# Two layers of attention and mixture on one core: the stage borders opened, and the closing norm moved into the attention's last stretch

## What is computed

```python
x = L0_attn_x                                    # [4, 1024, 256]
x = x + attn0(layernorm(x))                      # 16 heads, window of 64 keys, softmax, W_out
x = x + ffn0(layernorm(x))                       # softmax gate + bias over 8 experts, top 2, SwiGLU; 2 shared experts
x = x + attn1(layernorm(x))
x = x + ffn1(layernorm(x))                       # gate logits, 8 Sinkhorn rounds, each expert takes its top tokens

def attn1(x, ...):                               # here x is the normalised input
    Q, K, V = x @ wq + bq, x @ wk + bk, x @ wv + bv
    attn = softmax(Q @ K.T / 4)                  # heads by a reshape of [4*16, 1024, 16], all keys
    out = ctx @ wo + bo + x
    mu, var = mean(out), var(out)
    return (out - mu) * rsqrt(var + 1e-5) * gamma + beta
```

## Time and profile before

| what | us |
|---|---|
| median of 3 runs (lowest, highest) | 2432.5 (2428.86, 2436.8) |
| the profiled execution | 2439.18 |
| its span, first to last instruction | 2437.2 |
| TensorE busy | 2024.1 (83%) |
| VectorE busy | 1630.2 (67%) |
| ScalarE busy | 1116.2 (46%) |
| GpSimd busy | 452.3 (19%) |

### The profile page before, as it was taken

The page is one execution under the profiler, slowest core; times in us unless marked ns, Lnnn a source line. Parts: engine busy times, 40 slices in busy tenths (PEclk is TensorE's granted clock), DMA queues, the critical chain, the costliest instruction groups (busy, mean ns, idle before and its releaser), DMA issues. The chain is left out here.

```text
span 2437.2 us, 51300 instructions
## 1 busy us (share of the span) xinstructions
PE 2024.1 (83%) x18407; PEld 1393.6 (57%) x18408; DVE 1630.2 (67%) x2834; ACT 1116.2 (46%) x2169; POOL 452.3 (19%) x608
## 2 busy tenths in 40 slices
PE   2888888669979999989968899999999999835052
PEld 2766766448879999988857533434334343324042
DVE  3666666556735555546644579999999999386953
ACT  1555545333223333332223158888888888611010
POOL 2101001010011111114434112112221122030036
PEclk9999999889989999999989769999999999955566
DMA  2000000192151111113339777745755900031036
GB/s 87 2 0 0 0 0 0 60 336 80 35 182 47 47 47 47 47 43 106 109 114 271 201 51 72 67 46 52 49 47 47 71 2 2 5 104 35 0 112 200
DMA packets 207045, 172.15 MB, mean 71 GB/s; under 512 B 121740, under 2 KB 184808, under 8 KB 204744
## 3 DMA queue, kind: packets, MB, share of 16 engines
q1 hardware_dynamic: 187448, 131.64, 27.8%
q0 software_dynamic: 17744, 26.26, 4.0%
q10 hardware_dynamic: 1728, 12.58, 1.4%
HBM read 106.30 MB, written 63.84 MB: 70 GB/s over the span
## 5 line engine op out<-in xcount | busy, mean ns | idle before, releaser
L1811 DVE TENSOR_REDUCE ga_nmax<-banks 128x1 fp32r<-128x1024 f32 x512 | 615.5, 1219 | 39.8 <-PE banks L1890 38.4
L1845 ACT ACTIVATE ga_probT<-banks 128x512 f32<-128x512 f32 x1024 | 556.7, 597 | 157.6 <-PE banks L1903 105.9
L1890 PE MATMUL banks<-a_ks,a_qs 48*128 48x512 f32 x1024 | 392.3, 466 | 9.3 <-PEq L77 5.3
L1903 PE MATMUL banks<-a_qs,a_ks 49*128 49x512 f32 x1024 | 381.8, 453 | 0.0
L1920 PE MATMUL banks<-ga_probT,a_v 128*32 128x256 f32 x4096 | 332.9, 398 | 6.4 <-ACT ga_o L1851 6.4
L1890 PEld LDWEIGHTS banks<-a_ks,a_qs 48*128 48x128 f32 x1024 | 159.4, 195 | 225.2 <-DVE ga_nmax L1811 158.3
L1321 PEld LDWEIGHTS banks<-rb_xT,rb_own_w 128*128 128x128 f32 x2272 | 267.1, 193 | 8.3 <-issue 3.7
L1321 PE MATMUL banks<-rb_xT,rb_own_w 128*128 128x128 f32 x2272 | 267.9, 276 | 4.1 <-DMA rb_w<-in_L_ffn_rw_dram 3.5
L1790 POOL DMA_DIRECT2D a_qs<-ga_max_rows x256 | 130.8, 519 | 580.6 <-DVE ga_max_rows L1818 539.4
L1296 ACT ACTIVATE rb_silu<-banks,rb_own_b 128x128 f32<-128x128 f32 x284 | 80.9, 367 | 254.9 <-PE banks L1321 254.9
L1920 PEld LDWEIGHTS banks<-ga_probT,a_v 128*32 128x32 f32 x4096 | 81.6, 108 | 198.3 <-ACT ga_probT L1845 151.2
(11 more groups left out here) (288 smaller groups left out, 3031.7 us busy)
## 6 DMA issues: line engine op xcount, KB each, us to landing
m_xnT<-xnT_parts ACTq DMA_DIRECT2D x12, 1024.0 KB, 4.8
sorted_out<-rb_yb SPq DMA_DIRECT2D x71, 128.0 KB, 1.7
xnT_parts<-np_parts SPq DMA_DIRECT2D x8, 1024.0 KB, 9.2
m_w<-in_L_ffn_rw_dram SPq DMA_DIRECT2D x2, 4096.0 KB, 21.6
values<-pg_v SPq DMA_DIRECT2D x16, 512.0 KB, 3.1
a_v<-values SPq DMA_DIRECT2D x16, 512.0 KB, 9.1
a_qs<-queries_rounded SPq DMA_DIRECT2D x28, 256.0 KB, 8.5
a_ks<-keys_rounded SPq DMA_DIRECT2D x28, 256.0 KB, 9.6
```

The costliest lines, as they stand in the source:

```text
L1811: nc.vector.tensor_reduce(nmax[b % 2][:, at:at + 1], slot[:], axis=AX.X, op=ALU.max, negate=True).then_inc(use_read, 1)
L1845: nc.scalar.activation(probT[k % SETS][2 * h + n][:], b_t[ring_place["weights", w] % RING][:], ACT.Exp, scale=SCALE).then_inc(exp_ready, 1)
L1890: return nc.tensor.matmul(slot[:, HALF * kh:HALF * (kh + 1)], qs[a][rows, n, P * q:P * (q + 1)], ks[a][rows, n, HALF * kh:HALF * (kh + 1)] ...
L1903: nc.tensor.matmul(bank[:], ks[a][rows, 2 * gp + n, P * kt:P * (kt + 1)], qs[a][rows, 2 * gp + n, HALF * hf:HALF * (hf + 1)], start=True, ...
```

## The change

Nothing is computed in another way except the last gate; work and waits are placed elsewhere.

1. `setup` loses its stage: `window_attention` loads x (batch 0, then the qkv weights, then the other batches) and takes statistics of the first 8 tiles before its steps, of the other 24 in places 0 to 5 of step 0, and finishes them at place 6. The wide mask is made for one pair and copied. TensorE waits for the identity first, and for weights and masks where they are used.
2. `finish_stats` is gone. Its operations (`Closing`) stand at the start of `normalised_tiles`, `project_groups` and `gated_tiles`, and inside `group_attention`.
3. `normalised_tiles` writes the first two parts straight into the buffers of the next stage, and no longer waits for its writes; `shared_expert` 0 waits for them where it reuses memory (SP before it loads weights, VectorE before `gated`, ScalarE before `silus`).
4. The weights of `project_groups` are loaded during `shared_expert` 1.
5. In `group_attention` the statistics are taken right after each `project`. From step 512 on VectorE finishes those of 28 tiles, and in eight chosen steps does `new_x` (scale, multiply, add old x) and new statistics by four tiles; GpSimd adds beta. The old x is loaded into a free query buffer in blocks 27 to 31.
6. `gated_tiles` takes the place of `norm_residual`: it does the last four tiles, and then normalise, transposes, gate matmuls with the gate's 8 columns stationary and 512 tokens moving, and transposes of the logits.

```diff
@@ window_attention, SP, VectorE
+            load_x(0)
             sp.dma_start(wqkv[:], ...).then_inc(wqkv_in, 16)
+            for b in range(1, B):
+                load_x(b)
...
+            nc.vector.memset(eps[:], LN_EPS)
+            for t in range(TB):
+                tile_statistics(t)
+            finish(0, 0, TB)
             dve.wait_ge(w_hi, ONE + 1)
...
+                    if c == 0 and place < 6:
+                        for t in range(TB + 4 * place, TB + 4 * place + 4):
+                            tile_statistics(t)
+                    if c == 0 and place == 6:
+                        finish(1, TB, T)
@@ window_attention, ScalarE, TensorE
+                        if c == 0 and place == UP - 1:
+                            root(1, TB, T)
                         weights(r, c, place)
...
-            pe.wait_ge(w_in, ONE + 16 * HU * 2)
-            pe.wait_ge(w_cut, ONE + 1)
-            pe.wait_ge(consts_set, ONE + 1)
+            pe.wait_ge(ident_set, ONE + 1)
@@ normalised_tiles, SP
-                if i == 5:
-                    sp.wait_ge(parts_kept, ONE + 16 * 4)
-                    for s in range(2):
-                        shared.load_chunk(sp, xnT_out, s, s, chunks_in)
...
-            sp.wait_ge(chunks_in, ONE + 16 * 2)
-            sp.wait_ge(parts_kept, ONE + 16 * STEPS)
-            for u in range(2):
-                sp.wait_ge(rows_kept[u], ONE + 16 * (STEPS // 2))
@@ shared_expert, SP
+            if route is not None:
+                sp.wait_ge(shared.parts_kept, 16 * NC)
+                for kept in shared.rows_kept:
+                    sp.wait_ge(kept, 16 * NC // 2)
+            else:
+                sp.wait_ge(w_ready, ONE + 2)
+                project.load(sp, ins, routed_in)
@@ project_groups
-            dve.wait_ge(b_in, ONE + B_IN)
-            dve.wait_ge(v_one, ONE + 2)
+            closing.on_vector(dve)
...
-            act.wait_ge(b_in, ONE + B_IN)
+            closing.on_scalar(act)
...
-            pe.wait_ge(w_in, ONE + W_IN)
@@ group_attention
+        XB_AT, QUARTER = (27, 28, 30, 31), T // 4
+        NEW_AT = [UNITS + k for k in (3, 7, 14, 18, 22, 26, 30, 34)]
...
+            def new_x(i):
+                for t in range(4 * i, 4 * i + 4):
+                    nc.vector.scalar_tensor_tensor(g.x[:, t, :], g.x[:, t, :], g.mean[:, t:t + 1], gamma[:],
+                                                   ALU.subtract, ALU.mult).then_inc(scaled_ready, 1)
+                dve.wait_ge(xb_in[4 * i // QUARTER], ONE + 16)
+                dve.wait_ge(scaled_ready, ONE + 4 * i + 4)
+                for t in range(4 * i, 4 * i + 4):
+                    nc.vector.scalar_tensor_tensor(g.x[:, t, :], g.x[:, t, :], g.rstd[:, t:t + 1], kept_tiles(qs, t, 1)[:, 0],
+                                                   ALU.mult, ALU.add).then_inc(x_ready, 1)
+
+            def new_statistics(i):
+                dve.wait_ge(beta_ready, ONE + i + 1)
+                for t in range(4 * i, 4 * i + 4):
+                    nc.vector.bn_stats(g.stats[:, t, :], g.x[:, t, :])
...
-                        if arg >= LATE:
-                            dve.wait_ge(use_read, ONE + use + 1)
-                            statistics(arg)
-                if UNITS <= s < UNITS + LATE:
...
+                        dve.wait_ge(use_read, ONE + use + 1)
+                        for h in range(2):
+                            nc.vector.bn_stats(g.stats[:, t + 2 * h, :], g.x[:, t + 2 * h, :]).then_inc(stats_ready, 1)
+                if s == UNITS:
+                    dve.wait_ge(stats_ready, ONE + READY)
+                    closing.moments(dve, 0, 0, READY)
+                if s == NEW_AT[0]:
+                    dve.wait_ge(ends_in, ONE + 16 * 3)
+                    closing.inverses(dve, 0, 0, READY)
+                if s in NEW_AT:
+                    i = NEW_AT.index(s)
+                    if i < READY // 4:
+                        new_x(i)
+                    if i:
+                        new_statistics(i - 1)
...
+                if back == UNITS - LAG + 3:
+                    closing.on_scalar(act, 0, 0, READY)
...
+            for i in range(READY // 4):
+                pool.wait_ge(x_ready, ONE + 4 * i + 4)
+                four = g.x[:, 4 * i:4 * i + 4, :]
+                nc.gpsimd.tensor_tensor(four, four, beta[:].unsqueeze(1).broadcast_to([P, 4, D]), ALU.add).then_inc(beta_ready, 1)
@@ gated_tiles in place of norm_residual: VectorE, ScalarE, TensorE
+            closing.moments(dve, 0)
+            closing.inverses(dve, 0)
+            normalise(0)
+            normalise(1)
+            last_tiles()
+            closing.moments(dve, 1, READY)
+            closing.inverses(dve, 1, READY)
+            for i in range(2, STEPS):
+                normalise(i)
...
+                for k in range(KD):
+                    last = nc.tensor.matmul(b_g[i % 2][0:E, :], gw[:, k, :], xnT[i % 2][:, k, :], start=(k == 0), stop=(k == KD - 1))
...
+                for c in range(C):
+                    last = nc.tensor.transpose(b_l[i % 2][:, E * c:E * (c + 1)], lT[i % 2][:, P * c:P * (c + 1)], g.ident[0:E, 0:E])
...
+            for i in range(STEPS + 2):
+                if i < STEPS:
+                    transposes(i)
+                if 1 <= i <= STEPS:
+                    gates(i - 1)
+                if i >= 2:
+                    turned(i - 2)
```

488 lines of the change are left out of this document (258 added, 230 removed).

## The result

The changed kernel took 2353.2 us (median of four runs, 2347.5 to 2367.3) against 2434.7 for the kernel before (2428.9 to 2439.4): a ratio of 0.9681, 95% interval 0.9658 to 0.9704. That is 10 us more than the 81.5 between the medians: it sets the shortest of four runs after against one of the longest before.

The account below looks back on a forecast made before the run. It took TensorE and VectorE as nearly full in the score stage, and the closing norm and gate as a chain of waits. Terms -16 - 12 - 9 + 3 + 13.4 - 46 = -67 gave a median of 2366 us, range 2342 to 2386.

Parts of the forecast that it names:

- Start, -16: Kernel start: first qkv matmul 23 us earlier, 7 us given back in step 0; 16 us saved, between 12 and 20.
- Gate stage, -12: First mixture's gate stage: shared expert's first matmul at 517.5 instead of 529.33; 12 us saved, bounds 8 and 15.
- I take 3 us for the compute: First mixture's gate stage: 3 us saved in compute, part of SP's last issue ending at about 511 instead of 514.6.
- a wait that only moves behind this stage: First mixture's gate stage: SP's queue ends no earlier, ScalarE waits to 525; 8 of 12 us lost, 2374; chance 0.08.
- Projection stage, -9: Projection stage: weights already there, so VectorE's 9.97 us wait shrinks; 9 us saved, bounds 7 and 9.5.
- Score stage, +3: Score stage: added VectorE statistics delay scores by 0.2 us at 14 projections; 3 us lost, bounds 0 and 13.
- the slower rival: Score stage: late maxima keep TensorE's clock low for 160 us or more longer, losing at least 67 us; chance 0.03.
- Stretch without scores, +13.4: Stretch without scores: added new_x and statistics groups of 5.85 us make the last context late; 13.4 us lost, bounds 8 and 20.
- ScalarE's root costs it two table loads and itself, 2 x 1.28 + 0.3 = 2.9: Stretch without scores: the root takes 2.9 us of ScalarE, which sets the pace, putting projection 14 at 2101.3.
- Closing stage, -46: Closing norm and gate: last tiles, then six low-clock steps and a tail, ending at 2193; 46 us saved.
- I take the low one: Closing stage: TensorE stays at the low clock since most matmuls use 8 of 128 columns; steps of 5.7 us, 54 us stage.
- The rival with the high clock: Closing stage: TensorE gets the high clock, steps about 3 us instead of 5.7; 15 us less, 2351; chance 0.30.

Follow-up runs that it names:

- the run with three places: Changed kernel with the first window step's statistics at places 1, 3 and 5, eight tiles each, instead of four at places 0 to 5; 2355.0 us, ratio 0.9669.
- the run with narrow fillers: Changed kernel with six more 8-column gate matmuls, results unused, on TensorE in the closing stage; ratio 0.9660 to the kernel before.
- fillers of full height: Changed kernel with four unused 128x128 identity transposes in each of the score stage's first twelve units; ratio 0.9716 to the kernel before.
- root two steps sooner: Changed kernel with ScalarE's root in the stretch without scores two steps (four exponentials) sooner; stretch 67.97 us, ratio 0.9697 to the kernel before.

## Why the prediction came out as it did

**Start, -16.** Right: -18.6. The first matmul came 1.8 us sooner than worked out. The first step gave back 5.6 us: 0.9 and 1.8 in the first two pairs of places, 2.9 where the norm is finished; with 1.9 more by the stage's end it is 7.5, against 7. That a pair's second place hides its statistics, as the prediction had it, the run with three places bears out: with all of them there, the first three pairs take 6.51, 5.26 and 6.21 us, against 6.37, 4.92 and 6.37 before, and the step gains 1.2 to 3.3 us.

**Gate stage, -12.** -16.0, just outside the bound of -15. The gap behind SP's last issue came as worked out: 14.7 us before, 6.8 after (487.92 to 494.74), 6.5 in the forecast. The mis-sized term is "I take 3 us for the compute": SP's last issue ends 31.8 us behind the first normalisation in place of 39.9, so 8.1 us came from there, where the forecast had 3.6. The forecast's rival, a wait that only moves behind this stage, didn't come: SP's wait ends at 496.48, but TensorE began at 494.74 without it. Put back at its old place the wait costs 6.3 us.

**Projection stage, -9.** -6.8, and between -2 and -9 in the other profiled executions, since a first mixture of some 700 us lies in the same cut; right, within what these cuts can tell. A narrower cut, from the second shared expert's last matmul to the first normalisation behind it, leaves that mixture out: 18.95 us before and 10.52 in each execution after, 8.4 less.

**Score stage, +3.** The forecast had the wrong sign. The mis-sized term is "14 x 0.2: **+3**". The statistics cost nothing: from one projection to the next, a pair of blocks takes 43.53 us (1960.57 to 2004.10) against 43.64 before (2011.47 to 2055.11, whose end is in the earlier trace rows). The -9.6 come from the clock. In the earlier trace rows it was still 0.50 up to 1446, 69 us into the stage; after, it rose 45 us in:

```profile
1377.00:1381.00 4.00, 4.00 (x24) 1.18 (x24) 2.34 (x4) 2.17 (x4) 3.37 (x7) 0.50 0.99 56
1381.00:1410.00 29.00, 28.80 (x284) 10.77 (x280) 28.07 (x25) 25.34 (x47) 4.81 (x10) 1.00 0.78 58
```

The twelve profiled executions of the changed kernel and its variants without fillers in this stage give 41, 45, 45, 45, 45, 50, 52, 56, 58, 58, 73 and 75 us, with stages of 691.6 to 705.7: (705.7 - 691.6) / (75.4 - 41.1) = 0.41 us of stage per us of late rise, next to the 0.42 that the prediction worked out for the slower rival; the other ten lie within 0.3 us of this line. At 69 us it gives 703.1, and before took 702.6. So at an equal rise the added work is worth 0 (-0.5). The prediction took the 69 us of one execution for a property of the stage; that the changed kernel drew 45 is luck, worth 10 us.

**Stretch without scores, +13.4.** +20.2. The mechanism named (groups of 5.85 us, GpSimd's addition against VectorE's operations with two tensors as input, the root's 2.9 us) is all there: groups take 5.70, the collisions behind projection 14 4.1. The failed step is "ScalarE's root costs it two table loads and itself, 2 x 1.28 + 0.3 = 2.9": the pause starved TensorE, the clock fell, and projection 14 came 10 us late, where 2.9 were put. With the root out of ScalarE's way the stretch costs 56.1 - 45.9 = +10.2; the prediction's sum less its 2.9 for the root is +10.5. So the rest of it was right as far as the numbers tell, though it holds a slip: 2101.3 + 1.6 + 5 x 5.85 is 2132.2 and not 2131.3.

**Closing stage, -46.** -61.0. The failed step is the choice "I take the low one" for the clock. The norm and the last tiles took what they were given: from 2094.8 to the last tiles' normalisation at 2108.44 it is 13.6 us, against 15. From the third on the steps ran at 3.2 us, the number worked out for the high clock (about 3), and the stage came out at 40.6 us where that rival had 39. The argument from the earlier trace rows, that matmuls using part of the array don't raise the clock, is refuted: matmuls of 8 columns alone raised it, and padding them to 128 changed nothing. Nor did full transposes among the matmuls of 48 rows, over 22 us, raise it in the score stage. The Trainium skill ("TensorE: Matmul & The Clock Gate", section "What's actually happening") names sustained busyness as what releases the clock. The closing stage and the run with narrow fillers agree; the score stage, with TensorE busy for 5.00 of 5 us at a granted clock of 0.50, does not, and neither do the 53.10 busy us at 0.50 in the stretch.

**The sum.** The time lay in the range although two steps failed, and that is in part luck: the stretch cost 7 us more than forecast, the closing stage 15 and the score stage 12.6 less. The rival with the high clock, given 0.30, is what happened in the closing stage.

**What stays open.** Why the clock takes 41 to 75 us to rise at the start of the score stage, while it took 6 us at the start of the shared expert (0.50 at 494, 0.97 from 500) and 17 to 24, or 55, in the stretch. Full transposes in its first 20 us didn't bring the rise sooner, and neither did a shorter idle time ahead (3.51 us in place of 5.66); each is one profiled execution of a quantity that varies by 34 us. In all thirteen executions of the changed code the rise came behind the point, 32 to 39 us in, at which the transposed scores' matmuls join; whether that is a cause was not separated. Up to there TensorE was busy for 28.3 of 31.8 us, from there to the rise for 13.1 of 13.5 (changed kernel); with the fillers of full height it was busy for 20 of 20 us from 1335 to 1355. Open too is why 1.24 us of idle time were followed by a fall in the stretch, and 1.22 us not in the window attention.

## What to carry to other kernels

A pause on one engine costs its length plus what it does to the clock: a root with two table loads on ScalarE, 2.9 us, became 10 because TensorE starved for 2.3 us behind it and the clock fell; starving it for 1.2 us only was no better. A few dependent small operations on an engine that waits anyway (12 of 0.22 us) can be cheaper than one function on the engine that sets the pace. Read a stage's clock in several executions before its length is compared: here the same instructions took 692 to 706 us.

## What the runs showed of the hardware

- TensorE's granted clock fell to 0.5 behind an idle time of only 1.24 us, in the midst of a stage that was otherwise full, and stayed there for 24 us with TensorE busy throughout. In the window attention twelve idle times of 1.22 us, 25.5 us apart, left it at 1.00, as did those of some 0.2 us ahead of ScalarE's output copies.
- From one execution to the next, with the same instructions, the rise in the score stage came 41 to 75 us after its first maximum, and in the stretch without scores 17 to 55 us after the fall.
- The granted clock rose from 0.50 to 1.00 when TensorE had done nothing since its last idle time but transposes of 128x128 (2117 us, root two steps sooner), and when it had done nothing but matmuls of 8 columns by 512 (2103 to 2104 us, narrow fillers).
- Integer shifts and multiply-adds on 128x28 take VectorE 0.18 and 0.24 us, beside 0.17 to 0.19 for its float operations of that size.
- VectorE adds beta to 128x1024 in 1.22 us, GpSimd in 2.4, and beside GpSimd's addition four of VectorE's operations with two tensors as input took 3.76 us in place of 1.67; without that addition the groups took 4.66 us in place of 5.70.
- The second mixture took 238 to 241 us in the four executions on one chip and 210 to 213 in all others, with the same instructions; the cause was not looked for.
